# A four-layer graph network on one core: in the edge-weighted sums the weight moves from the gathered rows into the one-hots

## The reference, cut to what matters

```python
row, col = (edge_index[0], edge_index[1])
...
edge_weight = jax.nn.sigmoid(h @ mlp_w2 + mlp_b2)[:, 0]
...
deg = jax.ops.segment_sum(ew_f, col_f, num_segments=n)
dinv = jnp.where(deg > 0, jax.lax.rsqrt(deg), 0.0)
norm = dinv[row_f] * ew_f * dinv[col_f]
xt = x @ conv_w
msg = xt[row_f] * norm[:, None]
out = jax.ops.segment_sum(msg, col_f, num_segments=n)
return out + conv_b
```

## Time and profile before

| | |
|---|---|
| median of 3 runs | 6093.46 us (6088.32 to 6094.34) |
| the profiled execution's own time | 6093.4 us |
| its span, first to last instruction | 6091.6 us, 106746 instructions |
| PE busy | 4740.4 us (78%) |
| DVE busy | 3572.8 us (59%) |
| ACT busy | 4072.1 us (67%) |
| POOL busy | 4144.7 us (68%) |
| `weighted_sums` lies at | 2440.9 to 2830.4 us of the span |

### The profile page before, as it was taken

One profiled execution on the slowest core, in us unless ns is written; L12 is line 12 of the kernel. 1 busy time (PEld: TensorE's weight loads), 2 busy tenths in 40 slices (PEclk: granted clock), 3 DMA queues, 4 the chain that ended last, 5 costly groups with the idle time before them and its releaser, 6 DMA issues. The chain is left out here.

```text
span 6091.6 us, 106746 instructions
## 1 busy us (share of the span) xinstructions
PE 4740.4 (78%) x30944; PEld 3627.7 (60%) x30944; DVE 3572.8 (59%) x13039; ACT 4072.1 (67%) x7910; POOL 4144.7 (68%) x4218
## 2 busy tenths in 40 slices
PE   5666666659999999787899999699999845555555
PEld 3656666538888887777455555555555544444454
DVE  5777777753343334997544444344544446766665
ACT  3888888757777776997544444444444458888885
POOL 2777777547777777653777777477777737777773
PEclk9888888755555555999899999799999965555556
DMA  4444444215555555674222222122222223333332
GB/s 138 132 133 134 133 133 133 72 45 156 155 154 154 152 156 146 212 222 125 57 60 58 60 60 57 53 57 60 60 58 60 55 61 84 83 83 82 83 84 55
DMA packets 413318, 617.71 MB, mean 101 GB/s; under 512 B 88510, under 2 KB 266514, under 8 KB 412770
## 3 DMA queue, kind: packets, MB, share of 16 engines
q0 software_dynamic: 154368, 345.37, 21.7%
q1 hardware_dynamic: 255138, 264.52, 15.4%
q10 hardware_dynamic: 3264, 0.99, 0.1%
HBM read 530.85 MB, written 79.70 MB: 100 GB/s over the span
## 5 line engine op out<-in xcount | busy, mean ns | idle before, releaser
L1211 POOL DMA_INDIRECT sum_rows<-tab_row,src_idx x1496 | 1448.5, 968 | 604.5 <-issue 453.2
L1277 PE MATMUL sum_pX<-sum_mask,sum_part 128*128 128x512 bf16 x6174 | 1398.5, 381 | 0.0
L1238 ACT ACTIVATE sum_hot<-iota,local 128x128 f32<-128x128 f32 x1664 | 530.6, 389 | 873.6 <-PE sum_pA L1306 865.6
L642 POOL DMA_INDIRECT l_rows<-tab_qv,src_idx x832 | 791.7, 952 | 359.2 <-issue 247.3
L1359 DVE TENSOR_TENSOR acc<-acc,sum_pA 128x128 f32 x1664 | 474.8, 285 | 954.4 <-PE sum_pA L1306 926.9
L642 POOL DMA_INDIRECT l_rows<-tab_wh,src_idx x832 | 786.8, 946 | 345.0 <-issue 252.1
L374 POOL DMA_INDIRECT l_rows<-tab_ax,src_idx x832 | 819.0, 984 | 281.3 <-issue 253.2
L1277 PEld LDWEIGHTS sum_pX<-sum_mask,sum_part 128*128 128x128 bf16 x6174 | 607.2, 98 | 655.4 <-issue 9.3
L685 PE MATMUL l_pA<-l_hotA,l_wrow 128*128 128x128 f32 x3328 | 654.6, 359 | 97.9 <-ACT l_hotA L731 48.1
L727 ACT ACTIVATE l_hotA<-iota,local 128x128 f32<-128x128 f32 x1664 | 525.9, 386 | 201.0 <-PE l_pA L685 200.9
L685 PEld LDWEIGHTS l_pA<-l_hotA,l_wrow 128*128 128x128 f32 x3328 | 578.7, 262 | 116.9 <-ACT l_hotA L731 106.3
(11 more groups left out here) (299 smaller groups left out, 9410.5 us busy)
## 6 DMA issues: line engine op xcount, KB each, us to landing
l_line<-dst_at SPq DMA_DIRECT2D x312, 256.0 KB, 3.5
spill<-l_rows SPq DMA_DIRECT2D x104, 512.0 KB
sum_rows<-spill SPq DMA_DIRECT2D x104, 512.0 KB
sum_line<-src_lo SPq DMA_DIRECT2D x104, 256.0 KB
sum_rows<-tab_row,src_idx POOLq DMA_INDIRECT x1496
l_rows<-tab_qv,src_idx POOLq DMA_INDIRECT x832
l_rows<-tab_ax,src_idx POOLq DMA_INDIRECT x832
l_rows<-tab_wh,src_idx POOLq DMA_INDIRECT x832
```

Source lines behind the costliest of these rows:

```text
L642: nc.gpsimd.indirect_dma_start(rows[:, g % R, u, :], None, table, bass.IndirectOffsetOnAxis(src_idx[:, t:t + 1], 0)).then_inc(s_rows[g % R ...
L1211: nc.gpsimd.indirect_dma_start(rows[:, g % R, u, :], None, tab_row, bass.IndirectOffsetOnAxis(src_idx[:, t:t + 1], 0)).then_inc(s_rows[g % ...
L1238: last = nc.scalar.activation(hot[:, q % HOTS, u, :], iota[:], ACT.Square, scale=-1.0, bias=local[:, t:t + 1])
L1277: last = nc.tensor.matmul(pX[:, k % 2, :], part[:, i, h, :], mask[:, step % MASKS, :], start=h == 0 and i == 0, stop=h == NB - 1 and i == 2)
```

## The change: what it does

The weight of an edge goes into the one-hot of its target instead of into the row. `wrow` is gone: `sum_up` gives `rows` themselves to TensorE, and `hot` holds the weight where it held a 1. A weighted one-hot is made by one instruction per tile, TENSOR_SCALAR of 128x128 in fp32: `(iota == local) * wedge`, with both scalars read per partition. POOL makes tiles 1 to 7 of each batch, DVE (`own_onehots`, `OWN = 1`) makes tile 0. ACT no longer makes target one-hots; it makes the low one-hots `hot_lo` with a square and a Relu of 128x1024 each, and `low_onehot` on DVE is gone. A row buffer is now freed by `sum_up` (`s_sum`), no longer by POOL, and there are four of them; PE itself waits for the transfer. The semaphore `s_wedge` is now waited for by DVE too, and `s_hot` is split into `s_hot_pool` and `s_hot_dve`.

```diff
-                RB, LB, SB, Q = 3, 4, 3, 4
+                RB, LB, SB, Q = 4, 4, 3, 4
+                OWN = 1
...
-                wrow = sb(L + "wrow", [P, SB, TB, F], fp32, cx)
...
                             if n >= RB:
-                                sp.wait_ge(s_wrow, n - RB + 1)
+                                sp.wait_ge(s_sum, n - RB + 1)
...
-                            pool.wait_ge(s_wedge, n + 1)
-                            pool.wait_ge(s_rows[n % RB], 16 * (n // RB + 1))
                             if n >= SB:
                                 pool.wait_ge(s_sum, n - SB + 1)
-                            nc.gpsimd.tensor_tensor(wrow[:, n % SB], rows[:, n % RB],
-                                                    wedge[:, n % 2].unsqueeze(2).to_broadcast([P, TB, F]), ALU.mult
-                                                    ).then_inc(s_wrow, 1)
+                            pool.wait_ge(s_wedge, n + 1)
+                            for u in range(OWN, TB):
+                                t = n * TB + u
+                                last = nc.gpsimd.tensor_scalar(hot[:, n % SB, u, :], iota[:], local[:, t:t + 1],
+                                                               wedge[:, n % 2, u:u + 1], ALU.is_equal, ALU.mult)
+                            last.then_inc(s_hot_pool, 1)
...
-                            pe.wait_ge(s_hot, n + 1)
-                            pe.wait_ge(s_wrow, n + 1)
+                            pe.wait_ge(s_rows[n % RB], 16 * (n // RB + 1))
+                            pe.wait_ge(s_hot_dve, n + 1)
+                            pe.wait_ge(s_hot_pool, n + 1)
...
-                                    last = nc.tensor.matmul(pA[:, b, q, bass.ds(by[u], P)], wrow[:, b, u, :],
+                                    last = nc.tensor.matmul(pA[:, b, q, bass.ds(by[u], P)], rows[:, n % RB, u, :],
                                                             hot[:, b, u, :], start=False, stop=u % Q == Q - 1)
...
-                            for u in range(TB):
-                                t = n * TB + u
-                                last = nc.scalar.activation(hot[:, b, u, :], iota[:], ACT.Square, scale=-1.0,
-                                                            bias=local[:, t:t + 1])
-                            last.then_inc(s_square, 1)
+                            b = n % 2
+                            act_e.wait_ge(s_line[n % LB], 16 * (n // LB + 1))
+                            if n >= 2:
+                                act_e.wait_ge(s_look, n - 1)
+                            nc.scalar.activation(hot_lo[:, b], line[:, n % LB], ACT.Square, bias=minus_p[:]
+                                                 ).then_inc(s_square, 1)
                             act_e.wait_ge(s_square, n + 1)
-                            nc.scalar.activation(hot[:, b], hot[:, b], ACT.Relu, scale=-1.0, bias=one[:]
-                                                 ).then_inc(s_hot, 1)
+                            nc.scalar.activation(hot_lo[:, b], hot_lo[:, b], ACT.Relu, scale=-1.0, bias=one[:]
+                                                 ).then_inc(s_lo, 1)
...
+                        def own_onehots(n):
+
+                            if n >= SB:
+                                dve.wait_ge(s_sum, n - SB + 1)
+                            dve.wait_ge(s_wedge, n + 1)
+                            for u in range(OWN):
+                                t = n * TB + u
+                                last = nc.vector.tensor_scalar(hot[:, n % SB, u, :], iota[:], local[:, t:t + 1],
+                                                               wedge[:, n % 2, u:u + 1], ALU.is_equal, ALU.mult)
+                            last.then_inc(s_hot_dve, 1)
...
-                                dve.wait_ge(s_wrow, n - 1)
+                                dve.wait_ge(s_hot_pool, n - 1)
...
                                 if n < BATCHES:
                                     find(n, u)
+                                if 1 <= n <= BATCHES and u == 2:
+                                    own_onehots(n - 1)
                                 if n >= 3 and u % Q == 1:
                                     add(n - 3, u // Q, at[u // Q])
                             if n < BATCHES:
                                 weigh_edges(n)
-                            if n + 2 < BATCHES:
-                                low_onehot(n + 2)
```

More of the change, by code:

```diff
@@ L954, in weighted_sums @@
                 s_wedge = sem(cx, L + "s_wedge")
-                s_wrow = sem(cx, L + "s_wrow")
                 s_square = sem(cx, L + "s_square")
-                s_hot = sem(cx, L + "s_hot")
+                s_hot_pool = sem(cx, L + "s_hot_pool")
+                s_hot_dve = sem(cx, L + "s_hot_dve")
                 s_sum = sem(cx, L + "s_sum")
@@ L1040, in _ @@
                         for n in range(BATCHES):
-                            b = n % SB
-                            if n >= SB:
-                                act_e.wait_ge(s_sum, n - SB + 1)
-                            for u in range(TB):
-                                t = n * TB + u
-                                last = nc.scalar.activation(hot[:, b, u, :], iota[:], ACT.Square, scale=-1.0,
-                                                            bias=local[:, t:t + 1])
-                            last.then_inc(s_square, 1)
+                            b = n % 2
@@ L1109, in _ @@
                         c.link(nc.vector.tensor_copy(hi_f[:], hi_i[:]))
-                        low_onehot(0)
-                        low_onehot(1)
                         for n in range(BATCHES + 3):
```

## The result

The changed kernel takes 6300.78 us (median of 4 runs, 6291.8 to 6302.03) against 6093.9 us for the kernel before (4 runs): ratio 1.034, 95% interval 1.0328 to 1.0353. It is 207 us slower. The direction was forecast, the size was not: 6118 us were forecast, and the range ended at 6160.

The account below looks back on a forecast made before the run. DVE was taken to lead at 3.56 us a batch. 97 rounds x 0.21 = 20.4, early batches 7 x 0.54 = 3.8, end +0.55, start -0.6: +24 us on 6093.4, forecast 6118 us, range 6097 to 6160.

Parts of the forecast that it names:

- What bounds the kernel before: Phase weighted_sums: DVE leads at 3.56 us a batch, POOL and PE follow it, ACT is hardly faster.
- The part removed from DVE: DVE's low_onehot, 0.48 us: the offset load behind it keeps its 0.67 us, so removal gives back only 0.09, say 0.08.
- The part added to DVE: DVE's one 128x128 one-hot per batch, read from a 218 ns row: adds 0.13 us to the round, 3.61 without waiting.
- The wait at POOL: DVE's one-hot waits each batch for a POOL instruction to end: 0.16 us, between 0 and 0.41 at most.
- p: Length of one POOL one-hot: taken as 0.35 us, between undisturbed rows of 293 ns and 0.41 us.
- the rule that I took from the Trainium skill: A VectorE instruction in a two-port mode and a GpSimd instruction lock each other out for an instruction's whole length.
- the round forecast for DVE: DVE's time from wedge to wedge: 3.61 + 0.16 = 3.77 us, 0.21 more than before.
- rival D: POOL leads instead of DVE, from p about 0.53; with p = 0.57, 4.22 us a batch, 6173 us; chance 0.17.
- D's own formula, 7p + 0.23: POOL's time per batch for seven one-hots; POOL leads when it exceeds DVE's 3.61 us and its wait.
- The sign that the prediction named for this error: In the profile after, POOL without idle time behind its seventh one-hot would show that p was wrong.
- The Trainium skill's price for p: GpSimd best case, 1.8 cycles at 1.2 GHz per element; with 0.18 us fixed time, p = 0.37 and about 6128 us.
- Start, early batches, end: Seven early batches with keep work take 4.36 us, 0.54 more each; last POOL piece 2.45, +0.55; start about -0.6.

Follow-up runs that it names:

- e7: Kernel before, with only DVE's TENSOR_LOAD of the offsets moved behind the second add: 6083.59 us against 6093.83, ratio 0.9983.
- e2: Changed kernel with POOL making only two of its seven one-hots a batch, all matmuls kept: 6112.75 us (single run).
- e3: As e2, with DVE's TENSOR_LOAD of the next batch's offsets moved behind the second add: 6061.07 us (single run).
- e6: As e2, with four kinds of TENSOR_SCALAR of 128x128 on DVE in place of its one one-hot: 6169.81 us (single run).
- e5: Changed kernel with the compare in POOL's one-hots replaced by an add, so they hold wrong values: 6112.7 us (single run).
- e1: Changed kernel with seven different kinds of POOL instructions in place of its seven one-hots a batch: 6148.27 us (single run).

## Why the prediction was wrong

**What bounds the kernel before: right.** DVE leads at 3.56 us, with ACT just behind. e7 shows it: shorten DVE's round and the time falls, until ACT takes the lead at 3.52.

**The part removed from DVE: right.** Taking away `low_onehot` and its 0.48 us left the 0.66 us from `wedge` to the first `find` (e2), as the earlier trace rows had them, and only moving the load gave the time back (e3, -51.7 us). The Trainium skill, "DMA: Bandwidth & Descriptors", section "Latency and other measured facts", gives about 600 ns as the floor of a `tensor_load`. The trace agrees, with 0.66 us from the start of the instruction ahead to that of the one behind.

**The part added to DVE: wrong by a factor of two.** 0.13 us was taken and 0.26 measured. The row it was read from has a constant where the one-hot reads two scalars per partition, and e6 prices each at 60 ns. With 0.26 the forecast would have been 13 us higher.

**The wait at POOL: wrong.** 0.16 us a batch was forecast, from 0 to p. e2 is no test of it, for there DVE's one-hot starts when POOL's two are all but over. e5 is: POOL runs seven TENSOR_SCALAR, and DVE's one-hot starts in the middle of them.

```profile
2650.61 3.02 POOL L990 TENSOR_SCALAR sum_hot<-iota,local,sum_wedge 128x128 f32<-128x128 f32 x7 [0.72 <-DVE sum_wedge L1085]
...
2652.09 0.34 DVE L1062 TENSOR_SCALAR sum_hot<-iota,local,sum_wedge 128x128 f32<-128x128 f32 x1
```

A wait to the end of the POOL instruction would have made it some 0.2 us longer. In nine of ten batches of e5 it takes less than 0.36. In the kernel after, where POOL never stops, there are delays, but short ones: of the 99 one-hots beside POOL's TENSOR_SCALAR alone the middle one takes 0.39 us, three quarters are under 0.44, and the longest takes 0.57:

```profile
2704.46 0.34 DVE L1062 TENSOR_SCALAR sum_hot<-iota,local,sum_wedge 128x128 f32<-128x128 f32 x1
2969.57 0.57 DVE L1062 TENSOR_SCALAR sum_hot<-iota,local,sum_wedge 128x128 f32<-128x128 f32 x1
```

The waits that I had seen in the earlier trace rows were all beside a POOL TENSOR_TENSOR, and beside one they are there for the new instruction as well. From e2, an early batch:

```profile
2466.28 0.79 POOL L990 TENSOR_SCALAR sum_hot<-iota,local,sum_wedge 128x128 f32<-128x128 f32 x1
2466.98 1.82 DVE L1062 TENSOR_SCALAR sum_hot<-iota,local,sum_wedge 128x128 f32<-128x128 f32 x1
2467.04 1.68 POOL L995 TENSOR_TENSOR keep<-keep,dinv 128x896 f32<-128x896 f32 x1
```

So the rule that I took from the Trainium skill, "SBUF — State Buffer", section "Who interferes with whom", did not carry over to the new instructions: all five one-hots that met a `keep` TENSOR_TENSOR in the kernel after took 1.7 to 2.2 us, while POOL's TENSOR_SCALAR, with one tensor input and two scalars, delayed them by 0.23 us at the most. The Trainium skill's rule speaks of VectorE in a two-port mode, and whether the one-hot ran in one no trace shows; so why the two kinds differ stays open. The two errors, 0.13 too little and 0.16 too much, nearly cancel by luck: the round forecast for DVE was 3.77, and where DVE does lead (e2, e5) it is 3.72.

**p, the length of a POOL one-hot: the step that failed.** I took 0.35 us and bounded it at 0.41 undisturbed, 0.555 with disturbance, by a TENSOR_TENSOR that multiplies. It is 0.775 from start to start. That instruction has one input more, and I concluded that it bounds the one-hot from above; but it does not compare, and with an add in place of the compare the one-hot falls to 0.42 (e1, e5). With 0.775 in place of 0.35, POOL's seven need 5.43 us and rival D leads. D's own formula, 7p + 0.23, gives 5.66 and a time near 6325; the 0.23 us for a gap and for DVE's turn did not come. D had the right mechanism and was held at p = 0.57 by the same bound. Its first argument "for" was the one to follow: no row on POOL showed the operation at all. The sign that the prediction named for this error, no idle time behind POOL's seventh one-hot, is what the profile shows.

**The Trainium skill's price for p.** "GPSIMD Engine Reference", section "Elementwise — side-by-side cycle accounting", has 1.8 cycles per element as the best case, which I had turned into an estimate of 0.37 us. For add and multiply the measured 0.42 from start to start is near that; for the compare the measurement decides: 0.775, and 3.2 ns for each further column (e1), more than twice the 1.5 ns that 1.8 cycles at 1.2 GHz would be, an estimate from the same page.

**Start, early batches, end.** The early rounds were forecast at 4.36 us and are 7.06, and the last POOL piece is 5.4 us instead of 2.45: the same p. The start was right, 0.5 us sooner where 0.6 was forecast. That the transfers and the later freeing of buffers count as nothing was right too (e2).

## What to carry to other kernels

A bound from a neighbouring row is safe only if that row does the same operation; shape, type and number of inputs were not enough here on GpSimd, where one word (compare for add) nearly doubled an instruction. When no row of an engine shows the operation, leave the range open on the dear side, or count from the other end: here seven instructions in a round of 3.6 us could afford 0.5 us each. And before shortening an engine's work, look at what follows it in the same queue: because a register load hid under the instruction removed, taking 0.48 us away gave back only 0.09 until the load was moved.

## What the runs showed of the hardware

- GpSimd, fp32 TENSOR_SCALAR of 128x128 (e1, e5): add and multiply with two scalars per partition 447 ns, compare and multiply 791; compare alone 599; compare and multiply with constants 646. Multiply by one constant: 537.
- VectorE, the same shape (e6): 221 ns with two constants, 281 with one scalar per partition, 344 with two; with two scalars, compare and multiply or add and multiply alike.
- A VectorE TENSOR_SCALAR with two scalars per partition beside GpSimd's TENSOR_SCALAR: 0.34 us in most batches of e5, 0.34 to 0.57 in the kernel after. Beside a GpSimd TENSOR_TENSOR of 1.68 us: 1.7 to 2.2 us in the kernel after, 1.82 in e2.
- Two registers' TENSOR_LOAD on VectorE: the next instruction starts 0.66 us after the one ahead of the load has started, whether that one takes 0.17 us (e2) or 0.48 (the kernel before); behind one of 0.68 us the load costs nothing that can be seen (e3, e7).
